# Gated delta network layer: transposes of keys, values and outputs moved from TensorE to 32x32 turns and transfers through DRAM

## The reference

```python
mixed = silu(causal_conv(x @ w_qkv, conv_w))        # kernel of 4 taps
q, k, v = split(mixed)                              # 16 key heads, 32 value heads of 128
qf, kf = l2norm(q) * 128 ** -0.5, l2norm(k)
def step(state, q_t, k_t, v_t, g_t, b_t):
    state = state * exp(g_t)
    delta = (v_t - k_t @ state) * b_t
    state = state + outer(k_t, delta)
    return state, q_t @ state
o = outs * silu(z)
o = o * rsqrt(mean(o * o) + EPS) * norm_gamma
return o @ w_out                                    # 4096 -> 256
```

## Time and profile before

| | us |
|---|---|
| median of 3 runs | 1560.65 (1558.39 to 1560.72) |
| profiled execution: its span | 1560.0 |
| TensorE busy | 1401.0 (90%) |
| VectorE busy | 1005.2 (64%) |
| ScalarE busy | 785.7 (50%) |
| GpSimd busy | 694.3 (45%) |

### The profile page before, as it was taken

How to read it: one execution, slowest core, us unless ns; L and a number is a source line. 1 busy time by engine, 2 the same in 40 slices (tenths; PEclk the granted TensorE clock), 3 DMA queues, 4 the chain that set the end, 5 groups by cost and what they waited for, 6 DMA issues and landing times. The chain is left out here.

```text
span 1560.0 us, 26361 instructions
## 1 busy us (share of the span) xinstructions
PE 1401.0 (90%) x9528; PEld 993.8 (64%) x9528; DVE 1005.2 (64%) x2100; ACT 785.7 (50%) x1831; POOL 694.3 (45%) x1210
## 2 busy tenths in 40 slices
PE   6778899999999999999999999999898699789994
PEld 3456676766767667776767767677655356555672
DVE  5856777777776877877777777775522156451453
ACT  3445656565665756656575565655432256311121
POOL 1674664846648465573745638460100000016254
PEclk9878999999999999999999999999999899979997
DMA  3201111111111111111111111112100770013487
GB/s 92 56 18 39 28 40 37 39 29 34 39 38 30 38 35 39 25 42 31 42 38 21 39 39 37 30 21 54 52 1 0 300 186 1 25 68 108 97 177 158
DMA packets 127154, 86.72 MB, mean 56 GB/s; under 512 B 92403, under 2 KB 113095, under 8 KB 126257
## 3 DMA queue, kind: packets, MB, share of 16 engines
q1 hardware_dynamic: 120880, 76.50, 18.5%
q0 software_dynamic: 6144, 8.53, 3.0%
HBM read 61.65 MB, written 23.76 MB: 55 GB/s over the span
## 5 line engine op out<-in xcount | busy, mean ns | idle before, releaser
L1058 DVE SCALAR_TENSOR_TENSOR heads_y<-psum_banks,gdn_conv_w,heads_y 128x1021 f32<-128x1021 f32 (+2 forms) x192 | 245.2, 1278 | 26.5 <-ACT heads_y L878 24.4
L597 PE MATMUL psum_banks<-main_hT,gdn_w_in 128*128 128x512 f32 x512 | 250.8, 616 | 9.3 <-DVE heads_y L1058 3.9
L1331 POOL TENSOR_TENSOR heads_XT<-heads_XT,heads_tmp 128x126 f32<-128x126 f32 (+22 forms) x496 | 211.7, 427 | 38.9
L1328 POOL TENSOR_TENSOR heads_tmp<-heads_XT,heads_A 128x126 f32<-128x126 f32 (+22 forms) x496 | 184.1, 371 | 42.7 <-PE psum_banks L761 3.0
L597 PEld LDWEIGHTS psum_banks<-main_hT,gdn_w_in 128*128 128x128 f32 x512 | 94.4, 197 | 93.4 <-issue 77.0
L1309 POOL TENSOR_TENSOR heads_og<-heads_og,heads_fac 128x512 f32<-128x512 f32 x60 | 60.5, 1040 | 166.8 <-DVE heads_fac L1129 166.8
L707 PE MATMUL psum_banks<-heads_w_z,main_hT 128*128 128x256 f32 x512 | 125.4, 389 | 0.3 <-DVE heads_v_s L1148 0.3
L738 PE MATMUL psum_banks<-heads_w_o,heads_ogT 128*128 128x256 f32 x512 | 121.4, 387 | 3.6 <-ACT heads_ogT L944 3.6
L896 ACT ACTIVATE heads_O<-psum_banks,heads_coef 128x128 f32<-128x128 f32 x224 | 69.7, 363 | 92.6 <-PE psum_banks L628 91.3
L1866 POOL DMA_INDIRECT expert_rows<-moe_rows,route_dest x32 | 31.4, 981 | 189.9 <-DVE route_dest L1845 180.5
L878 ACT ACTIVATE heads_y<-psum_banks,gdn_conv_w 128x1024 f32<-128x1024 f32 x64 | 71.3, 1115 | 80.8 <-PE psum_banks L597 80.4
(11 more groups left out here) (275 smaller groups left out, 3102.4 us busy)
## 6 DMA issues: line engine op xcount, KB each, us to landing
main_w_gu<-in_w_gu SPq DMA_DIRECT2D x4, 2816.0 KB, 21.0
gdn_w_in<-in_w_in SPq DMA_DIRECT2D x16, 512.0 KB, 3.5
heads_A<-kk_blocks SPq DMA_DIRECT2D x64, 128.0 KB, 2.7
moe_wd<-in_w_down SPq DMA_DIRECT2D x32, 176.0 KB
expert_rows<-attn_zeros SPq DMA_DIRECT2D x1, 4624.0 KB, 29.9
moe_be<-expert_rows SPq DMA_DIRECT2D x32, 144.5 KB, 3.2
heads_w_z<-in_w_z SPq DMA_DIRECT2D x16, 256.0 KB, 2.7
heads_w_o<-in_w_o SPq DMA_DIRECT2D x16, 256.0 KB, 2.7
```

Source lines behind the costliest of these rows:

```text
L597: ins = pe.matmul(out[:, half * 512:(half + 1) * 512], w_in[:, kd_, j * P:(j + 1) * P], hT[:, kd_, half * 512:(half + 1) * 512], start=kd_ ...
L1058: dve.scalar_tensor_tensor(y[j][:, shift:T], src[:, 0:T - shift], conv_w[:, head, j, t:t + 1], y[j][:, shift:T], ALU.mult, ALU.add).then_i ...
L1328: pool.tensor_tensor(tmp[:, 0:n, 0:m], bc_last(XT[:, 0:n, j], m), bc_mid(A0[:, j, j + 1:BLK], n), ALU.mult).then_inc(solve_step.sem, 1)
L1331: pool.tensor_tensor(XT[:, 0:n, j + 1:BLK], XT[:, 0:n, j + 1:BLK], tmp[:, 0:n, 0:m], ALU.add).then_inc(solve_step.sem, 1)
```

## The change

Keys: VectorE turns all 32x32 blocks of `kT` in one instruction (128 x 1024 elements, `kt`, row 0). Four transfers store the blocks to DRAM in runs of 128 bytes, and four load them with tokens on partitions. Values: two turns (`vt0`, `vt1`, rows 5 and 6), four stores of 256 KB, one load of 1 MB, and then GpSimd multiplies with the key norm's factor (`scale_values`, 128 x 2048 elements, before it eliminates). Outputs, for heads up to step 16: two turns (`ot0`, `ot1`, rows 13 and 16), and for each four stores and one load of 512 KB in all. The output projection now keeps `w_o` stationary and streams the turned outputs, 512 tokens a product; its sum is kept with features on partitions, in the memory of `x`. After step 16 the sum is transposed once (16 tiles) and added to `x`, which is loaded again from DRAM. Gamma is multiplied into `w_o` by ScalarE. The last head still flips on TensorE.

The table `PLAN` is replaced by one table for each engine, with another order: `z2`, the decay products, `kk`, `attn`, `y6`, `u6` stand in other rows; `turn` goes from row 9 to row 7 and `scales` from row 12 to row 11.

```diff
-PLAN = [
-    [("z0", 0)],
-    [("p0", None)],
-    [("norm_q", 0), ("p1", None)],
-    [("z1", 3)],
-    [("k0", 1), ("k1", 2)],
-    [("v0", 1), ("v1", 2), ("v2", 3)],
-    [("p2", None), ("decay0", 3), ("decay1", 0), ("decay2", 1), ("decay3", 2)],
-    [("attn0", 1), ("p3", None)],
-    [("flip0", 0)],
-    [("kk0", 1), ("kk1", 3), ("v3", 2)],
-    [("y6a", 3), ("y6b", 0), ("z2", 2), ("p4", None)],
-    [],
-    [("u6a", 3), ("u6b", 0)],
-    [("p5", None)],
-    [("y7_0", 0)],
-    [("z3", 1)],
-    [("flip1", 2), ("attn1", 3), ("p6", None)],
-    [("p7", None), ("flip2", 1)],
-    [("y7_1", 2), ("u7_0", 0)],
-    [("flip3", 3)],
-    [("out0", 1)],
-    [("out1", 3), ("u7_1", 2)],
-    [("out2", 0), ("out3", 1)],
-]
-BANK = {name: b for row in PLAN for name, b in row}
...
+PE_PLAN = banked(rows("""
+0: z0/0
+1: p0/-1
+2: norm_q/0 p1/-1
+3: z1/3
+4: z2/2
+5: decay0/3 decay1/0 decay2/1 decay3/2
+6: p2/-1
+7: kk0/3 p3/-1
+8: kk1/0
+9: attn0/1
+10: attn1/2
+11: p4/-1
+12: y6a/3 y6b/0
+13: p5/-1
+14: u6a/3 u6b/0
+15: z3/1
+16: y7_0/0 p6/-1
+17: p7/-1
+18: y7_1/3 u7_0/0
+19: out0/2
+20: u7_1/3 out1/1
+21: out2/2
+22: out3/1
+"""))
...
+ACT_PLAN = rows("""
+0: z0 q_silu
+1: q_square v0_silu
+2: base0
+3: z1 v1_silu
+4: z2
+5: keys
+6: exp0 exp1
+7: exp2 exp3
+8: kk0 base1 kk1
+9: gamma
+12: norms y6a y6b
+14: base2 u6a u6b
+15: z3
+17: y7_0
+18: base3
+19: y7_1 u7_0
+21: u7_1
+""")
...
+DVE_PLAN = rows("""
+0: kt
+1: variance
+2: norm_q
+3: tap00 tap01
+4: tap02
+5: decay0 decay1 vt0
+6: decay2 decay3 vt1
+7: factors turn
+8: tap10
+9: tap11
+10: tap12
+11: scales attn0
+12: attn1
+13: ot0
+14: tap20
+15: tap21 tap22
+16: ot1
+18: tap30
+19: tap31
+20: inverse0 out0
+21: tap32 out1
+22: inverse1 out2 out3
+""")
...
+            def store_keys(h):
+                sp.wait_ge(kt_staged.sem, kt_staged.end(h))
+                wait(sp, kt_loaded, kt_loaded.base(h), 16)
+                for b in range(NB):
+                    src = flat(k_tok[h % 2][BLK * b:BLK * (b + 1)]).rearrange("p (n j) -> p n j", j=BLK)
+                    sp.dma_start(k_rows[:, :, b], src).then_inc(kt_stored.sem, 16)
+
+            def load_keys(h):
+                sp.wait_ge(kt_stored.sem, kt_stored.end(h) * 16)
+                for b in range(NB):
+                    sp.dma_start(flat(k_tok[h % 2][BLK * b:BLK * (b + 1)]),
+                                 k_rows[:, C * b:C * (b + 1)].rearrange("i c a j -> i (c a j)")).then_inc(kt_loaded.sem, 16)
+
+            def store_values(h):
+                sp.wait_ge(vt_staged.sem, vt_staged.end(h))
+                wait(sp, vt_loaded, vt_loaded.base(h), 16)
+                for b in range(NB):
+                    src = v_s[h % 2][BLK * b:BLK * (b + 1)].rearrange("p q e c j -> p q (e c j)")
+                    sp.dma_start(v_rows[:, :, b].rearrange("q i f -> i q f"), src).then_inc(vt_stored.sem, 16)
+
+            def load_values(h):
+                sp.wait_ge(vt_stored.sem, vt_stored.end(h) * 16)
+                sp.dma_start(v_s[h % 2][:].rearrange("p a e c j -> p (a e c j)"),
+                             v_rows.rearrange("q i a f -> (q i) (a f)")).then_inc(vt_loaded.sem, 16)
+
+            def store_outputs(h, u):
+                sp.wait_ge(ot_staged.sem, ot_staged.done(h, str(u)))
+                wait(sp, ot_loaded[u], ot_loaded[u].base(h), 16)
+                for b in range(NB):
+                    src = ogT[BLK * b:BLK * (b + 1), u].rearrange("p a i j -> p a (i j)")
+                    sp.dma_start(og_cols[u][:, :, b].rearrange("a i f -> i a f"), src).then_inc(ot_stored[u].sem, 16)
+
+            def load_outputs(h, u):
+                sp.wait_ge(ot_stored[u].sem, ot_stored[u].end(h) * 16)
+                sp.dma_start(ogT[:, u].rearrange("p q i j -> p (q i j)"),
+                             og_cols[u].rearrange("a i q f -> (a i) (q f)")).then_inc(ot_loaded[u].sem, 16)
+
+            store_keys(0)
+            load_keys(0)
+            store_values(0)
+            load_values(0)
...
                 if h in INVERT:
                     wait(sp, a_full, a_full.base(h))
                     sp.wait_ge(solve_step.sem, solve_step.end(h))
                     wait(sp, u_loaded, u_loaded.base(h), 16)
                     for s in range(2):
                         sp.dma_start(xd[:, :, :, s].rearrange("k b n i -> (k b) n i"), XT[64 * s:64 * s + 64]).then_inc(xd_stored.sem, 16)
+                    if h:
+                        load_keys(h)
                     if h == 0:
                         load_key_blocks(1)
                     sp.wait_ge(xd_stored.sem, xd_stored.end(h) * 16)
                     for b in range(NB):
                         r = slice(BLK * b, BLK * (b + 1))
                         sp.dma_start(Uf[h % 2][r, :, r], xd[:, b].rearrange("k n s i -> (n s) k i")).then_inc(u_loaded.sem, 16)
+                if h in INVERT and h:
+                    store_values(h)
+                    load_values(h)
                 if h in AHEAD and h:
                     key_block_stores(h)
                     load_key_blocks(h + 1)
+                if h in FINISH and h <= HK:
+                    store_outputs(h, 0)
+                    load_outputs(h, 0)
                 if h in SCAN and h < HK:
-                    sp.wait_ge(full[BANK["z3"]].sem, full[BANK["z3"]].done(h, "z3"))
+                    b = bank_of(h, "z3")
+                    sp.wait_ge(full[b].sem, full[b].done(h, "z3"))
                     weights("w_z", w_z_ready, h, w_z)
                 if h + 2 < HK:
-                    sp.wait_ge(full[BANK["decay3"]].sem, full[BANK["decay3"]].done(h, "decay3"))
+                    b = bank_of(h, "decay3")
+                    sp.wait_ge(full[b].sem, full[b].done(h, "decay3"))
                     gate_rows(h + 2)
+                if h in FINISH and h <= HK:
+                    store_outputs(h, 1)
+                    load_outputs(h, 1)
...
+                    if c == 0:
+                        pe.wait_ge(v_scaled.sem, v_scaled.end(h - 1))
                     for e in range(HD):
...
+                elif name == "out0" and h <= HK:
+                    pe.wait_ge(gamma_in.sem, gamma_in.end(h))
+                    pe.wait_ge(ot_loaded[0].sem, ot_loaded[0].end(h) * 16)
+                elif name == "out2" and h <= HK:
+                    pe.wait_ge(ot_loaded[1].sem, ot_loaded[1].end(h) * 16)
                 elif name == "out0":
...
+                elif name.startswith("out") and h <= HK:
+                    f = slice(P * (u % 2), P * (u % 2) + P)
+                    for e in range(HD):
+                        ins = pe.matmul(flat(bank[b][:]), w_o[:, e, f], ogT[:, u // 2].rearrange("p q (c e) j -> p e c q j", e=HD)[:, e],
+                                        start=e == 0, stop=e == HD - 1)
                     ins.then_inc(full[b].sem, 1)
...
+            def turn_sum():
+                for k in range(4):
+                    done = free[bank_of(HK, f"out{k}")]
+                    pe.wait_ge(done.sem, done.done(HK, f"out{k}"))
+                pe.wait_ge(b_free.sem, b_free.end(HK))
+                for u in range(4):
+                    for j in range(2):
+                        for f in range(KD):
+                            t = 2 * u + j
+                            ins = pe.transpose(ln_bank[u][:, 2 * j + f], sum_T[:, f, t * P:(t + 1) * P], ident[:])
+                    ins.then_inc(s_sum_turned, 1)
...
+                if name == "gamma":
+                    act.wait_ge(w_o_ready.sem, w_o_ready.done(h, "w") * 16)
+                    act.activation(flat(w_o[:]), flat(w_o[:]), ACT.Copy, scale=gamma[:]).then_inc(gamma_in.sem, 1)
...
+                if name == "kt":
+                    dve.wait_ge(k_ready.sem, k_ready.base(h))
+                    src = kT[h % 3][:].rearrange("p (c q j) -> p c q j", q=NB, j=BLK)
+                    dve.transpose(flat(k_tok[par][:]).rearrange("p (q c j) -> p c q j", q=NB, j=BLK), src).then_inc(kt_staged.sem, 1)
+                    return
+                if name.startswith("vt"):
+                    dve.wait_ge(act_ready.sem, act_ready.done(h, f"v{u}"))
+                    src = y[2 + u][:].rearrange("p (c q j) -> p c q j", q=NB, j=BLK)
+                    dve.transpose(v_s[par][:, :, u].rearrange("p q c j -> p c q j"), src).then_inc(vt_staged.sem, 1)
+                    return
+                if name.startswith("ot"):
+                    dve.wait_ge(normed.sem, normed.done(h, str(2 * u + 1)))
+                    src = og[par][:, C * u:C * (u + 1)].rearrange("p i (a j) -> p i a j", j=BLK)
+                    dve.transpose(ogT[:, u].rearrange("p a i j -> p i a j"), src).then_inc(ot_staged.sem, 1)
+                    return
...
+            dve.wait_ge(s_x_in, 16 * len(x_in))
+            dve.wait_ge(s_sum_turned, 4)
+            for u in range(4):
+                dve.tensor_tensor(flat(x[:, 2 * u:2 * u + 2]), x_in[u], flat(ln_bank[u]), ALU.add).then_inc(s_x_summed, 1)
+            dve.wait_ge(s_x_summed, 4)
...
```

(88 more changed lines are left out.)

272 lines of the change are left out of this document (142 added, 130 removed).

## The result

The changed kernel takes 1609.6 us (1605.9 to 1613.3) beside 1560.7 for the kernel before in the same runs: 1.031 times the time before, with an interval of 1.029 to 1.034. It is slower by 49 us. The forecast was 1544, in a range of 1504 to 1584.

A forecast was written before the change was run, and what follows sets the result against it. TensorE's list of work, coupled to VectorE, bounds the step. A full step changes by -4.9 + 3.6 = -1.3, thirteen by -17; with the other steps -16.5, 1560.0 becomes 1543.5 profiled, so 1544 us, range 1504 to 1584.

The forecast's parts named there:

- the stall: VectorE, and TensorE with it, stands at the block scales waiting for key blocks: 3.6 us per full step.
- TensorE's gain: 40 transposes at 0.11 us leave TensorE, plus 0.5 for waits: 4.9 us a full step (4.4 to 5.4).
- The chain from the last value turn to the key blocks: Value stores, value load, key-block loads and semaphores in SyncE's queue: 13.6 us, beside 10 us of VectorE's own work.
- rival C: Queue loses more than TensorE gains: chain over 14.9 us, stall over 4.9; 1571 at 5.5, 1595 at 7.2; chance 0.28.
- The lower bound: At the block scales: the value load does not hold the key blocks, kk1 decides, and the stall is 1.0 us.
- VectorE's turns: Turns of 32x32 blocks over 1024 columns on VectorE: 1.2 to 1.4 us each, five of them 6.0 us.
- GpSimd's product: Value scaling of 2048 columns before elimination: 4.1 to 4.7 us, hidden, ending at 14.2, before the scale factors at 14.5.
- The output products: Output projection on TensorE: same 4096 columns, same cost; moving operand read in runs of 32, priced at nothing.
- step 1: Pipeline step without outputs to flip: 3.1 us saved, 3.6 paid, +0.5.
- Step 15: Pipeline step without block scales: -4.9 less about 1.5 of waiting for the outputs, -3 us.
- step 16: Step of scan and outputs alone: turn, stores, load and semaphores make 9 us where 6.9 are available, +2.
- the tail: After the last step: 16 transposes of the sum and four adds, mostly under the wait for the last flips, +1 us.

The follow-up runs named there:

- e9: e1 with VectorE's block scales after attn0 in row 11 and GpSimd's value scaling in eight products instead of one: 1518.0 us, 0.971 times before.
- e3: The changed kernel without the value stores and load, GpSimd scaling the values as VectorE turned them (computation partly missing): 1531.2 us, 0.981 times before.
- e1: The changed kernel with the key-block stores and loads put ahead of the 1 MB value load in SyncE's queue: 1551.9 us, 0.994 times before.
- e10: The changed kernel with VectorE's block scales moved from row 11 to the end of row 13, ScalarE's norms to row 13: 1549.0 us, 0.991 times before.
- e8: e1 with GpSimd's value scaling as eight products of 256 columns instead of one of 2048: 1540.0 us, 0.985 times before.

## Why the prediction was wrong

Of the 62.6 us between the 1543.5 that was forecast for the profiled span and the 1606.1 that it took, the full steps hold 60. They are three terms of the sum, per step: the stall, 2.0 too small; the lower clock, 1.9, which had no term; and TensorE's gain, 1.2 too large (together 5.1, where the steps differ by 4.6). The mechanism of the stall, its place and its engine were as put.

- **The chain from the last value turn to the key blocks** is the step that failed first, as a size. In the step shown it was 16.05 us for 13.6, in the mean 16.6. The four value stores took 6.1 for 4.2: their four issues took 2.80 us, where I had taken those of the key-block stores, 1.78, and they landed 3.8 us after their issue, not 2.7. The load with the key-block stores behind it took 5.9 for 5.2, the key-block loads 4.0 for 4.1. VectorE's own work was 11.0 for 10. Stall 5.0 in that step, 5.6 in the mean, for 3.6: rival C, over its 4.9.
- **The price of standing still** was left out. "TensorE stands with it" was true, but the 1.9 us at the lower clock behind it were in no term and in no bound. The granted clock of 0.99 was read, but not that three steps of the kernel before pay 1.6 us each for it. If a stall of 3.6 us costs as much clock as one of 5.6, which no run shows, even the forecast stall leaves no gain: -1.3 + 1.9. Rival C at a stall of 5.5 was put at 1571; 13 x 1.9 us more would have made it 1596, outside the range.
- **TensorE's gain**, 4.9 a step and at least 4.4, was 3.7 with the waits cured: e9's step is 62.5, where the sum has 66.2 - 4.9 = 61.3. That is 16 us over the 13 steps, about as much as the whole gain that was forecast. The transposes themselves came to 4.2 us (819.9 of the earlier trace rows to 765.1 in e9, over 13) for 4.4; the 0.5 for waits between them did not come, e9 stands still 3.6 us a step where it was 3.1.
- **The sum by what was measured**: e9's 62.5, the stall 5.6 and the clock 1.9 make 70.0; the kernel after has 69.5. What hides the 0.5 is open.
- **The lower bound** (key blocks not held by the values, a stall of 1.0 from `kk1`): e3 measured 1.5, e1 1.6.
- **VectorE's turns**, 1.2 to 1.4 us: 1.23. Right. **GpSimd's product**, 4.1 to 4.7: shorter, 3.64, hidden in the stall and done (694.85) before the scale factors were (696.65), as said; with the stall cured it is not hidden (e1).
- **The output products** cost what a projection costs per column, 0.608 us a record and 0.605 before for a projection: no price for the strided operand, as taken. In full steps TensorE did not wait for loaded outputs, nor VectorE for the inverse blocks.
- **Outside the full steps**: step 1 had a stall of 8.6 for 3.6. Step 15 went from 54.7 to 54.3 (-3 was said), step 16 from 40.7 to 40.1 (+2). The steps ahead of step 2's variance grew by 8.4 and what follows the last variance fell by 4.9 (+1 was said for the tail); some 3 us of both are only that this instruction stands a row later now.

## What to carry to other kernels

Where one engine issues all transfers from one list, price a small transfer by what is ahead of it: the waits in the list, and what is still under way in the queue. 32 KB stores landed after 1.7 us alone and after 4.3 behind a 1 MB load, and moving them ahead of that load and its wait was worth 58 us of 1610. Give a wait of the engine that feeds TensorE its own row of slack, and count for each stall what the clock takes afterwards; look for the price in the trace at hand, in rounds that are longer than their neighbours at a lower granted clock. When one wait is cured, look again at once: here each cure uncovered a wait that had lain in the first one's shadow, and two edits worth 5 and 12 us alone were worth 34 together.

## What the runs showed of the hardware that I had not expected

- Four stores of 256 KB in runs of 2 KB took 2.80 us to issue, four loads of 128 KB 1.71.
- After 4.55 us without work TensorE ran at 0.55 of its clock for about 5 us. The length of the gap ahead does not tell it alone: after 1.33 us in e10 it fell in six steps and not in seven, and where it fell the step was 1.6 or 3.5 us longer.
- Beside one GpSimd product of 2048 columns (3.64 us) a VectorE product of 256 columns with both operands in SBUF took up to 3.6 us for 0.42; beside eight of 256 columns (4.81 us in all) at most 1.15 in e8 and 1.52 in e9.
- Over three times the traffic (121 GB/s for 37) did not lengthen a step (811.9 us for 13 in both).
